# Perceiver kernel, first cross-attention: half of the weighting dealt out behind three score steps, key products in another pair of PSUM banks

## The reference, cut to what matters

```python
q = (input_q @ wq).reshape(B, LQ, 16, 64).transpose(0, 2, 1, 3)
k = (input_k @ wk).reshape(B, LK, 16, 64).transpose(0, 2, 1, 3)
v = (input_k @ wv).reshape(B, LK, 16, 16).transpose(0, 2, 1, 3)
attn = softmax(einsum('bhqd,bhkd->bhqk', q, k) / sqrt(64))
out = einsum('bhqk,bhkd->bhqd', attn, v)
...
x = x + _L0_xattn_ref(_layernorm(x), ctx_1024, wq, wk, wv)     # the block of the change
```

## Time and profile before

| what | value |
|---|---|
| median of 3 runs | 973.45 us (971.85 to 974.96) |
| the profiled execution | 971.68 us |
| its span | 969.9 us |
| stretch of the first cross-attention's units | about 33 to 648 us |
| PE busy, share of the span | 97% |
| VectorE, ScalarE, GpSimd busy | 73%, 60%, 42% |

### The profile page before, as it was taken

One profiled execution on the slowest core, in us unless ns is written; L12 is line 12 of the kernel. 1 busy time (PEld: TensorE's weight loads), 2 busy tenths in 40 slices (PEclk: granted clock), 3 DMA queues, 4 the chain that ended last, 5 costly groups with the idle time before them and its releaser, 6 DMA issues.

```text
span 969.9 us, 31088 instructions
## 1 busy us (share of the span) xinstructions
PE 943.0 (97%) x13321; PEld 703.8 (73%) x13321; DVE 707.9 (73%) x900; ACT 583.1 (60%) x1404; POOL 410.5 (42%) x478
## 2 busy tenths in 40 slices
PE   6999999999999999999999999988989999999998
PEld 5666666666666666666666666667987787889998
DVE  4788888888878887888888888875025554467886
ACT  5667666666667666666667766642236663336664
POOL 2554445554555455454454545430113331513332
PEclk9999999999999999999999999999999999999999
DMA  6001111010000000000000000029838988408992
GB/s 234 25 24 25 25 24 25 24 25 24 24 24 24 25 24 24 15 13 25 24 24 24 25 24 3 4 80 401 287 145 269 280 273 301 174 2 297 319 337 95
DMA packets 78551, 98.07 MB, mean 101 GB/s; under 512 B 21584, under 2 KB 56928, under 8 KB 78432
## 3 DMA queue, kind: packets, MB, share of 16 engines
q1 hardware_dynamic: 77344, 94.67, 30.2%
q10 hardware_dynamic: 1088, 1.57, 0.5%
HBM read 95.68 MB, written 0.13 MB: 99 GB/s over the span
## 4 chain that ended last, share of the span: by engine, by line
PE 81%; DVE 7%; ACT 5%; issue 4%; POOL 2%; DMA 0%; ACTq 0%; DVEq 0%; POOLq 0%
PE ps L352 29%; PE ps L387 19%; PE ps L397 9%; PE ps L361 7%; PE ps L1583 6%; PE ps L1059 3%; PE ps L1600 2%; PE ps L1604 2%; PE ps L1601 2%; ACT x_pr L1225 2%; DVE c1T_lo L1263 1%; DVE x_negc L1269 1%; ACT c1T_hi L1219 1%; DVE x_negm L1272 1%; ACT x_prT L1233 1%
## 5 line engine op out<-in xcount | busy, mean ns | idle before, releaser
L562 ACT ACTIVATE probs<-ps,x_peak 128x512 f32<-128x512 f32 (+1 forms) x400 | 270.3, 679 | 186.6 <-DVE x_peak L657 180.5
L657 DVE TENSOR_REDUCE x_peak<-ps 128x2 f32<-128x1024 f32 (+1 forms) x200 | 232.8, 1201 | 47.4 <-PE ps L387 47.4
L676 DVE STREAM_TRANSPOSE probsT<-probs 128x1024 f32<-128x1024 f32 (+1 forms) x200 | 227.2, 1191 | 3.5 <-ACT probs L562 3.5
L852 POOL TENSOR_SCALAR vals<-vals_t,x_side 128x512 f32<-128x512 f32 (+1 forms) x100 | 152.8, 1540 | 127.9 <-PEq L404 127.9
L387 PE MATMUL ps<-keys,qT 64*32 64x512 f32 (+1 forms) x3200 | 204.4, 584 | 2.1 <-ACT keys L549 0.8
L352 PE MATMUL ps<-ctxT_hi,wk_hi 128*128 128x512 f32 (+1 forms) x400 | 160.7, 402 | 0.0
L352 PE MATMUL ps<-ctxT_hi,wk_lo 128*128 128x512 f32 (+1 forms) x400 | 154.9, 387 | 0.0
L352 PE MATMUL ps<-ctxT_lo,wk_hi 128*128 128x512 f32 (+1 forms) x400 | 154.5, 386 | 0.0
L549 ACT COPY keys<-ps 128x512 f32<-128x512 f32 (+1 forms) x200 | 115.4, 578 | 21.4 <-PE ps L352 10.3
L397 PEld LDWEIGHTS ps<-probsT,vals 64*32 64x32 f32 x6144 | 93.5, 105 | 32.9 <-issue 32.9
L352 PEld LDWEIGHTS ps<-ctxT_hi,wk_hi 128*128 128x128 f32 x400 | 75.0, 187 | 57.8 <-issue 40.2
(11 more groups left out here) (255 smaller groups left out, 1323.8 us busy)
## 6 DMA issues: line engine op xcount, KB each, us to landing
m_w<-in_m_w SPq DMA_DIRECT2D x32, 1024.0 KB, 7.6
ctx_raw<-in_ctxT SPq DMA_DIRECT2D x24, 512.0 KB, 4.0
ctx_two<-in_ctxT SPq DMA_DIRECT2D x24, 512.0 KB, 4.2
ctx_one<-in_ctx SPq DMA_DIRECT2D x24, 512.0 KB, 5.2
x_shrinkT<-x_shrink SPq DMA_DIRECT2D x384, 1.0 KB, 1.7
f_h1T<-in_f_h1T SPq DMA_DIRECT2D x1, 4096.0 KB, 18.1
f_h2T<-in_f_h2T SPq DMA_DIRECT2D x1, 4096.0 KB, 27.9
m_shared_w<-in_m_sw SPq DMA_DIRECT2D x2, 1024.0 KB, 9.5
```

The costliest lines, as they stand in the source:

```text
L562: return act.activation(m.probs[t % HALF][:, odd, 0:nt * P], m.ps[:, SCORE_BANKS[t % HALF] + odd, 0:nt * P], ACT.Exp, bias=m.peak[slot][:, ...
L657: dv.tensor_reduce(m.peak[slot][:, 1, cs, t % HALF], m.ps[:, bank:bank + 2, 0:nt * P], AX.X, ALU.min).then_inc(s["dve" if t == STEPS - 1 e ...
L676: i = dv.transpose(m.probsT[slot][:, cs, 0:4 * nt, t % HALF * 32:t % HALF * 32 + 32], m.probs[t % HALF][:, :, 0:nt * P].rearrange("p c (b ...
L852: t = gp.tensor_scalar(m.vals[slot][:, 0:4 * nt, cs, side * X0_DV:(side + 1) * X0_DV], m.vals_t[slot][:, 0:4 * nt, cs, :], m.side[:, side: ...
```

## The change

In a unit, `weighted` is cut into three parts of 3, 3 and 2 of its eight blocks (1, 2 and 1 of four behind the short chunk), issued behind score steps 0, 1 and 2. The key groups of `wide` go to banks 2 and 3, those of score step 1, and so their first one waits for that step's `scores_read`. The wait for `out_kept` and the signal `out_turned` move behind the second key group. On ScalarE the copy of the first key group moves from ahead of step 3's exponentials to between them, and that of the second behind them. On VectorE `turn_out` moves from behind the second maxima to behind the fourth. The first chunk keeps its banks 4 and 5 under the name `FIRST_BANK`.

```diff
-WIDE_BANK, VALUE_BANK, LAST_BANK = 4, 6, 4
+KEY_BANK, FIRST_BANK, VALUE_BANK, OUT_BANK = 2, 4, 6, 4
...
+    def output_turned():
+        pe.wait_ge(s["out_kept"], n("out_kept"))
+        pe.sem_inc(s["out_turned"], 1)
+
     def wide(slot, first_pair, half, nt):
 
+        pe.wait_ge(s["scores_read"], n("scores_read"))
         for q in range(HALF):
+            if q == 2:
+                output_turned()
             if q >= 2:
                 pe.wait_ge(s["k_kept"], n("k_kept"))
             key_group(slot, first_pair + q, nt)
-        pe.wait_ge(s["scores_read"], n("scores_read", 2))
+        pe.wait_ge(s["scores_read"], n("scores_read"))
         value_group(slot, half, nt)
...
-        for t in range(2):
+        of = range(2 * nt_before * half, 2 * nt_before * (half + 1))
+        cuts = (0, 3 * len(of) // 8, 6 * len(of) // 8, len(of))
+        for t in range(3):
+            if t == 2:
+                values_turned()
             scores(HALF * half + t, nt)
-        if half == 0:
-            pe.wait_ge(s["probs_turned"], n("probs_turned"))
-            pe.wait_ge(s["vals_ready"], n("vals_ready"))
-        weighted(1 - slot, range(2 * nt_before * half, 2 * nt_before * (half + 1)))
-        values_turned()
-        scores(HALF * half + 2, nt)
+            if t == 0 and half == 0:
+                pe.wait_ge(s["probs_turned"], n("probs_turned"))
+                pe.wait_ge(s["vals_ready"], n("vals_ready"))
+            weighted(1 - slot, of[cuts[t]:cuts[t + 1]], of)
         pe.wait_ge(s["scores_read"], n("scores_read"))
         scores(HALF * half + 3, nt)
-        pe.wait_ge(s["out_kept"], n("out_kept"))
-        pe.sem_inc(s["out_turned"], 1)
...
 (ScalarE, unit)
         for t in range(HALF * half, HALF * half + 3):
             exponentials(slot, t, CHUNK_TILES)
+        exponentials(slot, HALF * half + 3, CHUNK_TILES, first_pair)
         if first_pair is not None:
-            keep_keys(first_pair, CHUNK_TILES)
-        exponentials(slot, HALF * half + 3, CHUNK_TILES, None if first_pair is None else first_pair + 1)
+            keep_keys(first_pair + 1, CHUNK_TILES)
...
 (VectorE, unit)
-        for t in range(first, first + 2):
+        for t in range(first, first + HALF):
             maxima(slot, t, CHUNK_TILES)
         if half == 1 or order >= 2:
             dv.wait_ge(s["acc_added"], n("acc_added"))
         turn_out()
-        for t in range(first + 2, first + HALF):
-            maxima(slot, t, CHUNK_TILES)
```

More of the change, by code:

```diff
@@ L351, in key_group @@
             c = (m.c_hi, m.c_lo, m.c_hi)[term][slot]
-            done = pe.matmul(m.bank(WIDE_BANK + p % 2)[:, 0:nt * P], w[:, k, p * P:(p + 1) * P], c[:, k, 0:nt * P],
+            done = pe.matmul(m.bank(bank + p % 2)[:, 0:nt * P], w[:, k, p * P:(p + 1) * P], c[:, k, 0:nt * P],
                              start=(i == 0), stop=(i == TERMS - 1))
@@ L390, in scores, with weighted @@
         i.then_inc(s["scores_full"], 1)
-    def weighted(slot, blocks, quads=range(QUADS), signal="out_full"):
+    def weighted(slot, blocks, of, quads=range(QUADS), signal="out_full"):
         for b in blocks:
@@ L396, in weighted @@
                 for two, rows in enumerate((TOP, LOW)):
-                    i = pe.matmul(m.ps[32 * c:32 * (c + 1), WIDE_BANK + two, 0:P], m.vals[slot][rows, b, c, :],
-                                  m.probsT[slot][rows, c, b, :], start=(b == blocks[0]), stop=(b == blocks[-1]),
+                    i = pe.matmul(m.ps[32 * c:32 * (c + 1), OUT_BANK + two, 0:P], m.vals[slot][rows, b, c, :],
+                                  m.probsT[slot][rows, c, b, :], start=(b == of[0]), stop=(b == of[-1]),
                                   skip_group_check=True)
-        i.then_inc(s[signal], 1)
+        if blocks[-1] == of[-1]:
+            i.then_inc(s[signal], 1)
     def values_turned():
@@ L431, in unit @@
             wide(1 - slot, 0, 0, CHUNK_TILES)
+        else:
+            output_turned()
     def chunk(slot, nt_before, ahead):
@@ L464, in first_chunk @@
             pe.wait_ge(s["k_kept"], n("k_kept"))
-            value_group(0, half, nt, WIDE_BANK + half)
+            value_group(0, half, nt, FIRST_BANK + half)
         pe.wait_ge(s["scores_read"], n("scores_read", 3))
@@ L494, in last_output @@
         pe.wait_ge(s["vals_ready"], n("vals_ready"))
-        weighted(slot, range(4 * nt), (0, 1), "last_full")
+        weighted(slot, range(4 * nt), range(4 * nt), (0, 1), "last_full")
         pe.wait_ge(s["acc_whole"], 1)
@@ L509, in last_output @@
                 for two, rows in enumerate((TOP, LOW)):
-                    i = pe.matmul(m.ps[part:part + 32, LAST_BANK + two, P:2 * P], m.vals[slot][rows, b, c, :],
+                    i = pe.matmul(m.ps[part:part + 32, OUT_BANK + two, P:2 * P], m.vals[slot][rows, b, c, :],
                                   m.probsT[slot][rows, c, b, :], start=(b < 2), stop=(b >= 4 * nt - 2),
@@ L545, in split_context, with keep_keys @@
         act.copy(m.c_hi[slot][:, k, 0:nt * P], m.raw[slot][:, k, 0:nt * P]).then_inc(s["ctx_hi"], 1)
-    def keep_keys(p, nt):
+    def keep_keys(p, nt, bank=KEY_BANK):
         act.wait_ge(s["k_full"], n("k_full"))
-        act.copy(m.keys[:, p, 0:nt * P], m.bank(WIDE_BANK + p % 2)[:, 0:nt * P]).then_inc(s["k_kept"], 1)
+        act.copy(m.keys[:, p, 0:nt * P], m.bank(bank + p % 2)[:, 0:nt * P]).then_inc(s["k_kept"], 1)
     def keep_queries(half):
@@ L605, in first_chunk @@
             split_key_weights(half)
-        keep_keys(0, nt)
+        keep_keys(0, nt, FIRST_BANK)
         keep_queries(0)
         for p in (1, 2, 3):
-            keep_keys(p, nt)
+            keep_keys(p, nt, FIRST_BANK)
         act.wait_ge(s["wv"], 16)
@@ L624, in first_chunk @@
         for p in (0, 1):
[L625 removed]
+            keep_keys(p, CHUNK_TILES, FIRST_BANK)
         exponentials(0, 6, nt)
[L627 removed]
+        keep_keys(2, CHUNK_TILES, FIRST_BANK)
         exponentials(0, 7, nt)
@@ L646, in xattn0_scalar @@
     act.wait_ge(s["last_full"], 1)
-    act.copy(m.last_out[0:64, :, :], m.ps[0:64, LAST_BANK:LAST_BANK + 2, 0:P]).then_inc(s["last_kept"], 1)
+    act.copy(m.last_out[0:64, :, :], m.ps[0:64, OUT_BANK:OUT_BANK + 2, 0:P]).then_inc(s["last_kept"], 1)
     act.wait_ge(s["last_full"], 2)
-    act.copy(m.last_two[:, :, :], m.ps[:, LAST_BANK:LAST_BANK + 2, P:2 * P]).then_inc(s["last_kept"], 1)
+    act.copy(m.last_two[:, :, :], m.ps[:, OUT_BANK:OUT_BANK + 2, P:2 * P]).then_inc(s["last_kept"], 1)
 def xattn0_vector(dv, m, s, n):
@@ L734, in first_chunk @@
         for half in range(2):
-            turn_values(0, half, nt, WIDE_BANK + half)
+            turn_values(0, half, nt, FIRST_BANK + half)
         for t in (4, 5):
```

26 lines of the change are left out of this document (12 added, 14 removed).

## The result

| | before | changed |
|---|---|---|
| median | 973.93 us (971.85 to 975.87, 8 runs) | 977.00 us (975.89 to 978.25, 8 runs) |
| ratio | | 1.0032, 95% interval 1.0020 to 1.0043 |
| profiled execution, span | 971.68, 969.9 us | 978.08, 976.3 us |

The change makes the kernel 3.1 us slower. The prediction was 980 us, slower: the direction is right and the sum too large. In the changed kernel ScalarE's exponentials are L572, its drain L583, its copies L559; VectorE's `turn_out` is L699; PE's score steps are L394 and its weighting L404.

What follows compares the result with a forecast made beforehand. PE, busy 97% of the span, was taken as the bound, with two instruction stalls a pattern. Terms +5.3 (pattern), +1.4 (early units) and +0.2 (end) gave +6.9 us on 971.68, forecast 980 us, own range 977 to 984, with rivals 973 to 985.

Steps and rivals of the forecast that it cites:

- the pattern: Four consecutive units, claimed to take 51.78 us against 51.31, +0.47 each, times 11.25 patterns: +5.3 us.
- the early units: The two units behind the short chunk, claimed to go from 12.11 and 12.09 to 12.8 us each: +1.4 us.
- the end: Last unit: turn_out ahead of the last turning of probabilities, +0.45, against a stall some 0.3 us shorter: +0.2 us.
- Matmuls and junctions at nothing: PE's matmuls and score-to-weighting junctions, claimed to cost nothing more; upper bound 0.4 us a unit.
- First key group at 5.55 and 5.63: Key groups' start, claimed to wait for step 1's exponentials: +0.16 us in second-half units, +0.24 in first-half units.
- Copies: Third and fourth key groups wait for ScalarE's copies; plain units, all waits included, +0.32 and +0.39 us.
- Opening unit's stall gone: Late load at the weighting's end, claimed gone or under 0.2 us; opening unit 12.88 instead of 12.99 us.
- Second unit's stall: Late load in step 3, claimed 0.35 us earlier, bounds 0 and 0.65; unit 13.24 us, between 12.93 and 13.55.
- The faster one: Rival: release chain 0.2 to 0.3 us shorter, so no key group waits; -9 us, 964; chance 0.12.
- The stall goes altogether: Rival: second unit's late load vanishes, unit 12.78, pattern as before; 975 us, no difference to be told; chance 0.18.
- The stall stays: Rival: second unit's late load stays at 5.45 us, unit 13.55, pattern 52.1; 984 us; chance 0.15.

Runs made afterwards that it cites:

- e11: The changed kernel measured a second time with nothing altered; 976.42 us, ratio 1.0050.
- e8: e6 plus ScalarE signalling the first of step 1's two banks behind its exponential, PE's second key group waiting for the drain; 960.67 us, ratio 0.9879.
- e3: The kernel before with 32 idle semaphore instructions put once on PE ahead of the units; 970.23 us, ratio 1.0001.
- e10: e8 with 32 idle semaphore instructions put once ahead of the units, shifting the block borders by 32 places; 965.14 us, ratio 0.9942.
- e9: e8 with its weighting cut into 1, 3 and 4 of the eight blocks instead of 3, 3 and 2; 960.46 us, ratio 0.9891.
- e12: e8 with its weighting cut into 0, 4 and 4 blocks, nothing behind step 0; 965.62 us, ratio 0.9935.
- e4: The changed kernel with the first key group's copy back ahead of step 3's exponentials, the second between them; 969.94 us, ratio 0.9984.
- e7: Dealing alone: changed kernel with keys in banks 4 and 5, copies in old order, turn_out behind the third maxima; 979.83 us, ratio 1.0077.
- e5: The changed kernel with its last unit alone in the old order, weighting whole behind step 1; 977.07 us, ratio 1.0035.
- e6: The changed kernel with the edits of e4 and e5 together; 967.95 us, ratio 0.9952.
- e2: The kernel before with 64 idle semaphore instructions a unit between the key groups' matmuls on PE; 1138.9 us, ratio 1.174.

## Why the prediction was right in direction and too large

**The direction is in part luck.** The sum was +6.9 us, of which +5.3 for the pattern, +1.4 for the early units and +0.2 for the end. The two profiled spans gave +1.2, +1.4 and +1.8, and e11 gave +0.1, +1.4 and +1.9. The term that carried the forecast nearly vanished, and one that it had at almost nothing took its place. With the end at +0.2 these sums would be 1.7 and 2.8 us, under the 2.9 us that the prediction itself calls no difference.

**Matmuls and junctions at nothing:** right, step 3 starts at 4.34 us for 4.36.

**First key group at 5.55 and 5.63 (+0.16, +0.24):** measured 5.55 and 5.63. e8 shows the cause: with the earlier release it starts at 5.39 to 5.41.

**Copies:** plain units predicted at 12.78 and 12.88, mean 12.79 and 12.86. The split was off: the third group came at 8.45 and 8.52 instead of 8.57 and 8.65, because the 0.1 us for "a load that is not hidden" didn't come on top (its load and its matmul both start at 365.26). The fourth came at 9.95, as predicted, held by the second copy; so it was that wait, to which I gave 0.01 to 0.02, that added 0.11 to 0.13.

**Opening unit's stall gone:** right, 12.87 in the mean for 12.88.

**Second unit's stall: this term was mis-sized.** In seven of the eleven second units the last load of step 3 comes 0.36 to 0.66 us behind the one before it, in the others less; the forecast had some 0.6 in each. "I take the middle, 0.35" gave 13.24; the eleven units are 12.77 to 13.22, mean 12.95, at the lower bound of 12.93. I placed the start of the fetch, the 16 KB transfer of an instruction block, where PE enters the block before, and argued that "the issue runs some way ahead of PE, so it may be less". The means over the eleven second units, in us from the unit's start, show it the other way about:

| kernel | PE at the border | PE 64 instructions before it | transfer starts | minus border | minus 64 before |
|---|---|---|---|---|---|
| before | 2.18 | 1.74 | 2.98 | 0.80 | 1.24 |
| e3, before shifted | 1.96 | 0.87 | 2.21 | 0.25 | 1.34 |
| changed, e8 (3, 3, 2) | 1.53 | 1.10 | 2.40, 2.35 | 0.87, 0.82 | 1.30, 1.25 |
| e10, shifted | 1.31 | 0.87 | 2.21 | 0.90 | 1.34 |
| e9 (1, 3, 4) | 2.18 | 1.09 | 2.38 | 0.20 | 1.29 |
| e12 (0, 4, 4) | 2.18 | 1.74 | 3.02 | 0.84 | 1.28 |

The last column is steady, the one before it isn't. A distance of 48 instructions would spread it over 0.85 to 1.22 us, one of 72 over 1.33 to 1.73. So the sequencer runs about 64 instructions ahead of PE there, and what counts is the place 64 ahead; the change moved that by 0.64 us, and the transfer came 0.58 earlier. The upper bound was the right end. The distance was fitted to the first five rows (e8 and changed as one) and tested by e12 alone, whose order up to the border is that of the kernel before. The other kernels dealt 3, 3 and 2 (e4 to e7, e11) have their transfers at 2.37 to 2.57 us, 1.27 to 1.47 behind the same place. Why the delay takes that long wasn't tested. The Trainium skill ("Advanced Engine Details and Errata", Engine Queue Depths) gives TensorE a queue of 64 instructions, "complicated with tiling". The matmuls here are tiled, and the trace agrees with 64 as the distance. At 11.25 patterns the 0.29 us is 3.3 of the 4.1 us by which the pattern term (+5.3 for +1.2) was too high. The rest is that I took the pattern of before as 51.31, from eight, where eleven give 51.34, and hundredths in the other units.

**Early units, +1.4:** right.

**The end, +0.2: too small**, measured +1.8. I counted `turn_out` on VectorE and left out that PE's own wait for `out_kept` stands ahead of the last weighting, with no key group to hide it. e5 moves that start back by 1.7 us. By e4 the wait alone costs 1.2 us of the 1.8. The low clock makes the 128 matmuls 1.1 us longer (5.2 for 4.1), of which 0.6 reach the next part (18.84 for 18.26 in e4); by e4 the wait doesn't always bring it, by e5 it can come without that wait.

**The rivals.** The faster one fell: the release chain is what the rows said. "The stall goes altogether" is nearest, nearer than the forecast: with 12.95 it goes by five sixths; the early units and the end then make the 3 us. "The stall stays" fell: in e12 it costs up to 1.3 us and moves with the fetch. The Trainium skill ("Runtime: NRT & Kernel Launch", instruction fetch mechanics) says that crossing a block is mostly hidden. In the kernel before, the trace agrees for five of the seven blocks of a pattern, which show no stall, and not for the two of the late loads (0.71 and 0.91 us in the rows).

## What to carry to other kernels

When matmuls go to a buffer that another engine reads, look at which instruction releases it: a signal behind the first half of a pair was worth 7.3 us here (e8 against e6), more than the whole change moved. Two changes that each cost (banks alone 1.0284, dealing alone 1.0077) can be near even together (1.0032), so price them together. At the last turn of a loop ask again what hides each wait. Where an engine runs through a block of 256 instructions as fast as here (due in 2.3 us before the change, in 2.9 after it), judge an order by when the sequencer, not the engine, reaches the border.

## What the hardware showed unexpectedly

- In the second units the transfer of an instruction block starts, in the mean, 1.24 to 1.34 us after PE is 64 instructions ahead of the border, in six orders of code; over all kernels dealt 3, 3 and 2 it is up to 1.47 (e6).
- An idle semaphore instruction on PE costs some 60 ns of issue (e2), and 64 a unit make the issue the bound of 24 large matmuls.
- The granted clock fell to 0.50 about the end of an idle time of 2.5 us in two executions of the changed kernel and stayed at 1.00 behind the same idle time in e4. About the end of a pause of 1.46 us it fell in e5, and of 1.45 us in e8; behind one of 1.47 us in e6 it stayed at 1.00.
